# A decoder block on one core: gate and norm waits reordered, and a second score and ready exponentials ahead of the value matmuls

## The reference

```python
x = x + attn(layernorm(x))            # q, k, v, o projections with biases, causal softmax
n = layernorm(x)
x = x + mha(n, ctx_2048, ctx_2048)    # 16 heads, causal softmax, keys = values = context
n = layernorm(x)
logits = einsum('bsd,ed->bse', n, W_gate)
rw = softmax(top_k(logits, 2)[0])
x = x + relu(n @ W_up.T) @ W_down.T + sum(rw) * (n @ W_expert)
```

## Time and profile before

| | us |
|---|---|
| median of 3 runs | 722.11 (721.55 to 724.09) |
| the profiled execution | 721.66 |
| its span, first to last instruction | 719.6 |
| PE busy | 677.8 |
| ACT busy | 501.0 |
| DVE busy | 498.8 |
| POOL busy | 257.8 |

### The profile page before, as it was taken

One profiled execution on the slowest core, in us unless ns is written; L12 is line 12 of the kernel. 1 busy time (PEld: TensorE's weight loads), 2 busy tenths in 40 slices (PEclk: granted clock), 3 DMA queues, 4 the chain that ended last, 5 costly groups with the idle time before them and its releaser, 6 DMA issues.

```text
span 719.6 us, 13877 instructions
## 1 busy us (share of the span) xinstructions
PE 677.8 (94%) x4488; PEld 523.9 (73%) x4488; DVE 498.8 (69%) x1730; ACT 501.0 (70%) x1450; POOL 257.8 (36%) x391
## 2 busy tenths in 40 slices
PE   7998999999999999999969987999989999899998
PEld 6776777767877677677756765777768777577786
DVE  6568666756766676767788789867887669564632
ACT  5678877767876677788899887676688657774110
POOL 3745545333555345751654424433211012000100
PEclk9999999999999999999999998999999999999999
DMA  9663433345433464355956685543363444510101
GB/s 316 171 156 77 125 82 89 75 115 146 117 77 89 117 178 117 84 123 132 273 123 166 158 232 120 148 109 96 88 174 91 113 99 104 141 45 1 58 1 58
DMA packets 52326, 86.12 MB, mean 120 GB/s; under 512 B 8608, under 2 KB 16800, under 8 KB 52256
## 3 DMA queue, kind: packets, MB, share of 16 engines
q1 hardware_dynamic: 52256, 85.25, 45.4%
HBM read 27.55 MB, written 7.34 MB: 48 GB/s over the span
## 4 chain that ended last, share of the span: by engine, by line
PE 77%; DVE 11%; ACT 6%; issue 2%; DMA 2%; POOL 1%; SPq 0%; ACTq 0%; POOLq 0%; DVEq 0%
PE t L480 15%; PE m L519 14%; PE m L520 13%; PE m L521 13%; PE pv L513 10%; PE s L466 8%; DVE probs L680 4%; ACT probs L908 3%; DVE prob L690 1%; DVE xT_lo L766 1%; ACT prob L917 1%; PE m L480 1%; DMA stack<-stage 1%; POOL probs L1021 1%; PE m L583 1%
## 5 line engine op out<-in xcount | busy, mean ns | idle before, releaser
L680 DVE CUSTOM_DVE_ANT_0 probs<-s,mask 128x128 f32<-128x128 f32 (+3 forms) x512 | 245.8, 482 | 135.2 <-PE s L466 132.9
L908 ACT ACTIVATE probs<-probs,negmax 128x128 f32<-128x128 f32 (+3 forms) x512 | 284.7, 559 | 44.6 <-DVE negmax L680 43.3
L480 PE MATMUL t<-ident,probs 128*128 128x128 f32 x1143 | 203.6, 276 | 12.1 <-ACT prob L917 5.0
L917 ACT ACTIVATE prob<-t 128x512 f32<-128x512 f32 (+1 forms) x232 | 125.3, 541 | 109.0 <-PE t L480 108.8
L466 PE MATMUL s<-stack 96*128 96x128 f32 (+3 forms) x512 | 197.5, 392 | 3.8 <-DMA stack<-stage 2.2
L1021 POOL TENSOR_SCALAR probs<-probs,rsum 128x128 f32<-128x128 f32 (+3 forms) x256 | 133.4, 539 | 181.8 <-DVE rsum L694 181.8
L480 PEld LDWEIGHTS t<-ident,probs 128*128 128x128 f32 x1143 | 144.6, 141 | 62.2 <-issue 7.8
L466 PEld LDWEIGHTS s<-stack 96*128 96x128 f32 x512 | 97.4, 190 | 16.5 <-DMA stack<-stage 3.0
L908 ACT ACTIVATION_READ_ACCUMULATOR probs<-probs,negmax 128x1 f32 x512 | 99.1, 194 | 0.0
L690 DVE COPY prob<-t 128x128 f32<-128x128 f32 (+1 forms) x217 | 76.7, 353 | 30.7 <-PE t L480 29.8
L519 PE MATMUL m<-xT_hi,w_lo 128*128 128x512 f32 x192 | 78.4, 409 | 0.9 <-DVE xT_lo L748 0.9
(11 more groups left out here) (144 smaller groups left out, 955.0 us busy)
## 6 DMA issues: line engine op xcount, KB each, us to landing
stack<-stage SPq DMA_DIRECT2D x384, 128.0 KB, 2.3
xt<-in_x SPq DMA_DIRECT2D x16, 256.0 KB, 4.7
xres<-in_x SPq DMA_DIRECT2D x4, 1024.0 KB, 5.9
kraw<-in_ctxT SPq DMA_DIRECT2D x16, 256.0 KB, 3.1
cv<-in_ctx SPq DMA_DIRECT2D x16, 256.0 KB, 3.2
x<-xres SPq DMA_DIRECT2D x3, 1024.0 KB, 5.4
res<-x SPq DMA_DIRECT2D x8, 256.0 KB, 6.3
out<-res SPq DMA_DIRECT2D x2, 1024.0 KB, 4.8
```

Source lines behind the costliest of these rows:

```text
L480: mm = nc.tensor.transpose(dst[:, chunk(qb - kb)], probs[:, (2 * P + h) % 3, OFF[qb] + PART * kb:OFF[qb] + PART * kb + PART], ident[:, :])
L680: nc.vector.tensor_tensor_reduce(probs[:, (2 * P + h) % 3, OFF[qb]:OFF[qb + 1]], score_tile(P, i), mask[:, T - N:T], -SCALE, BIG, ALU.add, ...
L908: nc.scalar.activation(tile, tile, ACT.Exp, bias=negmax[:, P % 2, h, qb:qb + 1], scale=-1.0, accum_out=total).then_inc(p_exp, 1)
L917: nc.scalar.activation(prob[kb][:, 2 * (P % 2) + h, :], turned_tile(P, i), ACT.Copy).then_inc(t_act, 1)
```

## The change

No instruction is added or taken away; instructions move. The engines' programs have the same work before and after. The parts are these.

1. In `plan()`, the fourth transpose of the next batch's x, ("L", b, 3), goes from slot 0 to slot 1 of the steps 4, 12 and 20, and ("O", 0, 3) and ("O", 1, 3) likewise from slot 0 to slot 1 of steps 12 and 20. Slot 0 of an even step is the one with the value matmuls.
2. `ahead(s)` is true for the even steps 26 to 42. In them PE does the second score of the next pair before the fills and the value matmuls, and ACT does the exponentials that have no need of the turned tiles before its first copy.
3. `turn` of a cross pair waits for the four exponentials one by one, where it waited for the last of them.
4. POOL waits, before its key halves, until the four norms of the step are done (`ln_done`, `f_ln`), in steps 36, 42, 44, 50, 52, 58 and 66.
5. The statistics of layer norm 5 go from step 34 (all four) to steps 32 and 34 (two each), those of layer norm 6 from slots 344, 345, 348, 349 to 339 to 342.
6. `FEED` of batches 0 and 1 is four slots later (344 and 408 instead of 340 and 404), so that their up, expert and down products are four slots later as well; the transposes "FL" stand closer together (offsets 1, 2, 4, 5 instead of 1, 3, 5, 7), and their last is three slots before the gate. The gate takes first its four matmuls with `xT_hi`, two in each slot, which wait for `fl_hi`, and then the four with `xT_lo`.

```diff
-FEED = tuple(PAIRS * (PAIRS * (f + B + 1) + 2) + 4 + 4 * (f // 2) for f in range(B))
+FEED = tuple(PAIRS * (PAIRS * (f + B + 1) + 2) + PAIRS for f in range(B))
...
+def ahead(s):
+
+    return s % 2 == 0 and 2 * CROSS_AT[0] - 2 <= s < feed_start(0) // PAIRS
...
-        return [z + 24, z + 25, z + 28, z + 29]
-    return [z + 16, z + 16, z + 17, z + 17] if j == B + 1 else [z, z, z + 1, z + 1]
+        return [z + 19, z + 20, z + 21, z + 22]
+    return [z, z, z + 16, z + 16] if j == B + 1 else [z, z, z + 1, z + 1]
...
-                    put(("L", b, t), PAIRS * b - 5, 4 + t + t // 3, 1)
+                    put(("L", b, t), PAIRS * b - 5, 4 + t + 2 * (t // 3), 1)
...
-                put(("O", b, t), PAIRS * (b + 1) + 1 + t, 4 if t < 2 else 0, 4)
+                put(("O", b, t), PAIRS * (b + 1) + 1 + t, (4, 4, 0, 1)[t], 4)
...
-                put(("FL", f, m), 0, u + 1 + 2 * m, 1, 1)
+                put(("FL", f, m), 0, u + 1 + m + m // 2, 1, 1)
...
-                if kb == 0 and not own(P // 2):
-                    pe.wait_ge(p_exp, PAIRS * P + NT * (h + 1))
...
+                    elif kb == 0:
+                        pe.wait_ge(p_exp, PAIRS * P + NT * h + qb + 1)
...
-                    pe.wait_ge(fl_lo, KC * n + c + 1)
...
-                    nc.tensor.matmul(dst, g_both[:, c, :], xT_lo[:, c, :], start=(c == 0), stop=False)
-                    mm = nc.tensor.matmul(dst, g_both[:, c, :], xT_hi[:, c, :], start=False, stop=(c == KC - 1))
+                    done, x_part = (fl_hi, xT_hi) if c < KC // 2 else (fl_lo, xT_lo)
+                    for k in (2 * c % KC, 2 * c % KC + 1):
+                        pe.wait_ge(done, KC * n + k + 1)
+                        mm = nc.tensor.matmul(dst, g_both[:, k, :], x_part[:, k, :], start=(c == 0 and k == 0),
+                                              stop=(c == KC - 1 and k == KC - 1))
...
-                    if 0 <= s + 1 < NP:
+                    if 0 <= s + 1 < NP and not (ahead(s) and i == 1):
                         scores(s + 1, i)
+                    if ahead(s) and i == 0:
+                        scores(s + 1, 1)
...
-                    if own((s + 1) // 2):
+                    if ahead(s) and i == 0:
+                        if other(s // 2):
+                            exped(P, k)
+                        exped(s + 1, 0)
+                        if own(s // 2):
+                            exped(s + 1, 1)
+                    elif own((s + 1) // 2) and not (ahead(s) and i == 1):
                         exped(s + 1, i)
                     if 0 <= s < NP and i in T_ACT:
                         turned(s, i)
-                    if other(P // 2) and not own((s + 1) // 2):
+                    if ahead(s) and other(s // 2) and i < 3:
+                        if i == 1:
+                            exped(s + 1, 1)
+                    elif other(P // 2) and not own((s + 1) // 2):
                         exped(P, k)
...
+                for j in range(B + 1, 2 * B):
+                    if s == norm_slots(j)[-1] // PAIRS:
+                        pool.wait_ge(ln_done, NT * (j + 1))
+                for f in range(B):
+                    if s == f_norm_slots(f)[-1] // PAIRS:
+                        pool.wait_ge(f_ln, NT * (f + 1))
```

## The result

| | before | changed |
|---|---|---|
| median, us | 722.98 (4 runs) | 714.48 (713.68 to 717.31, 4 runs) |
| the profiled execution | 721.66, span 719.6 | 713.75, span 711.9 |
| PE, DVE, ACT busy | 677.8, 498.8, 501.0 | 676.5, 494.2, 501.8 |

The ratio is 0.989, with a 95% interval from 0.9855 to 0.9926: the kernel is faster by about 8 us in this comparison. A second, longer series (10 runs of the changed kernel, 15 of the one before) gave 714.46 us and 0.9914 (0.9888 to 0.994), about 6 us. The time lies in the predicted range and 2 us from the forecast, but it did not come about as forecast.

The account below looks back on a forecast made before the run. It took the kernel for a TensorE matmul stream, busy 677.8 of 719.6 us, with about 42 us of holes. Terms -3.4, -1.3, -2.6, -1.0 and -1.4 gave -9.7 us, so 712.0, median 712.5; range 706.5 to 718.5.

Parts of the forecast that it names:

- Part 1: Steps 4, 12, 20: fourth transpose and output projection go behind the value matmuls, closing PE holes; -3.4 us (-2.2 to -4.35).
- the new wait in slot 4: Steps 4, 12, 20: the transpose's bank is emptied one slot later, so its next user waits; 0.3 us for each step.
- Rival (d): Steps 4, 12, 20: bank waits return in slot 4 at full size, the rest cancels; 720.5 us, chance 0.07.
- Part 2: Even steps 26 to 42: second score and ready exponentials go first, filling ACT's waits; -1.3 us for steps 26 to 39.
- the price of the early score: PE-bound even steps: the early second score waits for DVE's maximum and holds PE's queue; 0.5 us in all.
- the 0.45 of step 40: Step 40: gain from doing the second score and ready exponentials first; 0.45 us.
- Part 3: Steps 40 to 43: GpSimd waits for the norms and statistics move earlier, saving DVE time; -1.7 us (0 to -3.5).
- away from the tiles that the gate waits for: Steps 43 to 42: moving the next batch's statistics leaves DVE the same work, clear of the gate's tiles.
- Part 4: Steps 44 to 60: later feed-forward, gate in two halves; -0.94 in step 44, -1.0 in 50 to 52, -1.4 in 58 to 60.
- rival (a): Whole kernel: only PE-bound parts pay, holes filled in 353 to 454 us reopen next step; -4.5, 717.6 us, chance 0.20.
- rival (c): Nine even steps: the early score costs more than all gains, PE standing 10.4 us if in each; 729.7 us, chance 0.03.
- three signs of being wrong: Scores waiting over half a microsecond in many even steps, PE idling as long in steps 33 to 43, slow stretches elsewhere.

Follow-up runs that it names:

- exps_only: The changed kernel with the second score back behind the value matmuls, ACT's early exponentials kept; median 711.87 us, ratio 0.9897.
- exps_late: The changed kernel with the early second score taken back and the statistics of layer norm 6 in their old slots; median 711.24 us, ratio 0.9881.
- slots_only: The kernel before with only the fourth x transposes and output projections moved to slot 1 of steps 4, 12, 20; median 714.08 us, ratio 0.9928.
- no_ahead: The changed kernel with ahead(s) false for every step, so neither early score nor early exponentials; median 713.83 us, ratio 0.9911.
- late_stats: The changed kernel with the statistics of layer norm 6 back in their old slots; median 712.70 us, ratio 0.9901.

## Why the prediction held, and where it did not

**Part 1, -3.4 forecast, -4.7 measured.** The mechanism was right, and the value matmuls start 0.23 us behind the first score:

```profile
150.82 0.30 PE L471 MATMUL s<-stack 96*128 96x128 f32 x1
151.05 2.36 PE L518 MATMUL pv<-prob,V 128*32 128x512 f32 x32
```

Mis-sized was the new wait in slot 4, 0.3 for each step: there is none, in step 12 PE is busy 11.87 of 11.87. (Rival (d) is mis-added as well: with 3 x 0.72 taken off the 4.35, it gives 719.9 and not 720.5.) And step 4 gained 1.36 where the sum had 1.07, because a wait of 0.55 us for the same xT_lo, further back in that step of the kernel before, went too. I had looked only at the step's head.

**Part 2, -1.3 forecast for steps 26 to 39, 0.0 measured.** The failed step is the price of the early score, 0.5, with a row that said 1.16 for step 42 taken as an exception. It costs 2.1 us in steps 24 to 39. The exponentials and what else moved in these steps bring 2.1 there, near the 1.8 of the sum (0.8 + 0.5 + 0.5), so this side was right, and so was the 0.45 of step 40 (7.42 us to 7.01). In step 42, 0.81 and 0.86 us of the 1.16 stand in the traces. The row on which the price rested was right; I counted it in too few steps: the second score waits for its maximum 1.63 us in step 34, 0.46 in step 36 and 0.57 in step 38.

```profile
361.90 0.38 PE L471 MATMUL s<-stack 96*128 96x256 f32 x1 [1.63 <-DVE negmax L689]
```

Step 34 lost nothing by it, since its value matmuls wait 1.38 us for ACT's copy anyway, in before and in exps_only. And the wait is not the whole price. In steps 26, 28 and 32 the second score waits 0.07 us at most, and still these steps are 0.17, 0.29 and 0.33 us longer, and back at their old lengths in exps_only: its place ahead of the value matmuls puts them, and all that follows from them, off. Step 32, PE and then ACT:

```profile
347.09 0.75 PE L471 MATMUL s<-stack 96*128 96x128 f32 x2
347.77 2.36 PE L518 MATMUL pv<-prob,V 128*32 128x512 f32 x32
...
350.76 0.60 ACT L926 ACTIVATE prob<-t 128x512 f32<-128x512 f32 x1 [0.80 <-PE t L485]
```

That copy waited 0.80 us where I had 0.35, since the value matmuls began 0.68 instead of 0.23 behind the first score. The rule that spoke against the early score is that of the Trainium skill, "TensorE: Matmul & The Clock Gate", section "Step-by-step: what each phase is for", that matmuls stay in program order. The trace agrees with it: the value matmuls of step 38 began at 392.39, behind the score at 391.38, 1.89 us behind the first score, where in exps_only they had all that they needed after 0.99.

**Part 3, -1.7 forecast for steps 40 to 43 and -0.94 for step 44; the first trace shows +0.8 and -0.3, the second -0.1 and -0.7.** The second trace has the granted clock of before in steps 40 to 43, so the 1.7 is missing there by more than the clock. The step that failed by the runs is that moving the statistics is "away from the tiles that the gate waits for" and otherwise free: they now stand ahead of maxima for which PE waits, 0.62 and 1.02 us, and taking them back brought step 43 from 12.2 or more to 10.4 at a like clock. The norms went from 1.037 us to 0.52, so 2.0 us of DVE time were saved as worked out. Whether they came through, because "in step 42, where DVE is the bound", stays open. Against it: in the trace of before, part of DVE's 10.56 us was norms stretched into time in which it had little else to do, as the next scores stood behind value matmuls at half clock; behind short norms, and again at half clock, it idles for 1.69 us in exps_late and 2.05 in the changed kernel; taking the wait of POOL out alone cost 0.4 us with a scatter of 0.6. For it: at a clock of 1.00, slots_only has DVE busy for 10.30 of 10.33 us in step 42, and PE waits 0.35 and 0.60 us for its maxima; in no_ahead, at 1.00 too and with short norms, these waits are gone and the step took 9.38, but there transposes have left the step and statistics have come in as well. A run with the wait of POOL as its one difference from slots_only, and traces of both at 1.00, would decide it. The Trainium skill, "SBUF — State Buffer", section "🔬 SBUF: two separate sides", says that DVE in some modes and GpSimd take a port pair in turns, for a whole instruction each; the halving of the norms agrees with it.

**Part 4, -2.4 forecast with step 44's 0.94 aside, -1.5 measured.** Steps 50 and 58 at 9.13 are as worked out (9.1), step 51 lost 0.26 of 0.5, step 52 0.72 of 0.94, step 59 grew by 0.98 instead of 0.2. The sum had let the gate's wait vanish; about 1 us of it went ahead of the transposes one step earlier, where 0.57 us had stood, and ACT's part is the 0.74 behind it (0.19 before):

```profile
609.72 0.66 PE L539 MATMUL m<-ident,f_xln 128*128 128x128 f32 x4 [1.52 <-DVE xT_lo L775]
...
613.07 0.33 PE L485 MATMUL t<-ident,probs 128*128 128x128 f32 x1 [0.74 <-ACT prob L926]
```

Step 60 lost 3.18 in the trace, near the 2.9 of the sum, but 1.6 of that was a fall of the clock that slots_only, with the same wait, did not have. Against a trace at clock 1.00 steps 58 to 60 grew, from 29.31 to 29.99. I also put the gain and the loss in 58 to 60 down to one edit, when they belong to two.

**The clock.** I expected it to rise where the holes went. Over steps 40 to 43 it fell:

```profile
409.89:448.18 38.29, 30.38 (x211) 21.85 (x209) 30.11 (x109) 27.52 (x84) 13.86 (x16) 0.82 0.62 162
```

```profile
416.44:453.94 37.50, 30.17 (x219) 22.45 (x217) 32.79 (x111) 28.44 (x88) 10.15 (x12) 0.91 0.64 166
```

The first is steps 40 to 43 of the changed kernel, the second steps 40 to 43 of the one before (up to the first score of step 44). Over its 10 runs the changed kernel had a mean clock of 0.9903, the one before 0.9930; by the slope that is 1.4 us given back out of 6.8. Which hole does it stays open: exps_only has 0.9905, no_ahead 0.9940, late_stats 0.9925, and no single part orders them.

**The whole.** The forecast was -9.6 from 722.11. The steps that the change touches gave -5.8 with the end, the long series -5.7, at equal clock -6.8, so the forecast gain was 3 to 4 us too large. That the time still came within 2 us was luck. The forecast started from 722.11, the median of three runs, and 48 later runs of the same kernel have 720.12; the changed kernel has 714.48 in its first 4 runs and 714.46 in 10. A start 2.0 us too high made up for half of the gain that did not come. In size the result is nearer to rival (a), "only the PE-bound parts pay" (-4.5), than to the forecast, with part 1 larger than in it. In mechanism it is rival (a) only in part. (a) has each hole that is filled in 353 to 454 us open again in the next step, but exps_only shows that the exponentials did pay, 1.8 us in steps 32 to 39; what took it back was the early score, the mechanism of rival (c), at 2.1 us and not at its 10.4. Of the three signs of being wrong, two came and one came in part: PE idled 14.3 us in steps 33 to 43 (14.6 before), a slow stretch reached into step 41 in the first trace (0.88, before 1.00), and in three even steps (34, 38, 42) a score waited for its maximum by more than half a microsecond. The range, which reached into (a), was what was right.
